# Regrouping the shared expert of a decoder layer into units of 320 and 384, with a warm-up and finer first loads

## The reference

```python
yg = xf @ shared_gw.T                      # shared expert, hidden size 704
y, g = jnp.split(yg, 2, axis=-1)
shared = jax.nn.silu(g) * y @ shared_dw.T
scores = jax.nn.sigmoid(xf @ gate_w.T)     # 8 experts, top 2 per token
for e in range(N_EXPERTS):                 # hidden size 352 each
    gu = xf @ up_w[e].T
    g_e, u_e = jnp.split(gu, 2, axis=-1)
    out = out + (silu(g_e) * u_e) @ down_w[e].T * we[:, None]
return shared + out
```

## Time and profile before

| | us |
|---|---|
| median of 3 runs | 1063.21 |
| the runs | 1061.88, 1063.21, 1064.40 |
| time of the profiled execution | 1066.47 |
| its span, first to last instruction | 1064.7 |

### The profile page before, as it was taken

The page is one execution under the profiler, slowest core; times in us unless marked ns, Lnnn a source line. Parts: engine busy times, 40 slices in busy tenths (PEclk is TensorE's granted clock), DMA queues, the critical chain, the costliest instruction groups (busy, mean ns, idle before and its releaser), DMA issues.

```text
span 1064.7 us, 20098 instructions
## 1 busy us (share of the span) xinstructions
PE 1019.2 (96%) x6978; PEld 905.5 (85%) x6978; DVE 704.2 (66%) x1454; ACT 524.1 (49%) x1033; POOL 530.5 (50%) x515
## 2 busy tenths in 40 slices
PE   6999888999999999999999999999999899999996
PEld 5866667899999999999999999999887788778785
DVE  4277776777777777767767767767786364455447
ACT  5355545555455455455455455455543245556510
POOL 0156866763643643643643644644572644454452
PEclk9999999999999999999999999999999999999999
DMA  8100104424323223233223333224210869999742
GB/s 294 60 31 2 60 16 138 150 111 149 120 111 115 98 109 114 97 108 114 99 107 114 101 107 112 101 107 150 93 69 1 333 253 370 395 380 380 279 134 83
DMA packets 44696, 153.45 MB, mean 144 GB/s; under 512 B 3704, under 2 KB 3704, under 8 KB 41568
## 3 DMA queue, kind: packets, MB, share of 16 engines
q1 hardware_dynamic: 42400, 145.38, 38.2%
q0 software_dynamic: 2240, 7.34, 2.1%
HBM read 130.04 MB, written 22.66 MB: 143 GB/s over the span
## 4 chain that ended last, share of the span: by engine, by line
PE 71%; POOL 4%; DVE 4%; issue 3%; ACT 1%; another core or an unknown queue 1%; POOLq 0%; DVEq 0%; ACTq 0%
PE xa_y_ps L86 6%; PE xa_y_ps L88 5%; PE xa_y_ps L87 5%; PE ex_raw_ey_ps L2092 5%; PE ex_raw_gu_ps L86 4%; PE ex_raw_gu_ps L88 4%; PE ex_raw_gu_ps L87 4%; PE xa_c_ps L1880 4%; PE xa_c_ps L1876 3%; PE xa_c_ps L1875 3%; PE xa_turn_ps L1957 3%; PE xa_turn_ps L1913 3%; PE front_k_ps L86 3%; PE front_k_ps L88 3%; PE front_k_ps L87 3%
## 5 line engine op out<-in xcount | busy, mean ns | idle before, releaser
L1221 POOL TENSOR_TENSOR xa_probs<-xa_probs,xa_inv_sum 112x750 f32<-112x750 f32 x63 | 97.9, 1553 | 75.6 <-DVE xa_inv_sum L1548 75.6
L1497 DVE TENSOR_TENSOR xa_kT_lo<-xa_turn_ps,xa_kT_hi 128x750 fp32r<-128x750 f32 x63 | 59.2, 940 | 99.9 <-ACT xa_kT_hi L1309 99.8
L1206 POOL TENSOR_TENSOR k_ms<-k_ss,sum_eps 125x6 f32<-125x6 f32 x63 | 12.6, 200 | 210.7 <-DVE k_ss L1513 210.7
L1875 PE MATMUL xa_c_ps<-xa_probsT_hi,xa_nat 125*128 125x224 f32 x384 | 92.3, 274 | 2.7 <-ACT xa_probsT_hi L1325 2.7
L1876 PE MATMUL xa_c_ps<-xa_probsT_hi,xa_nat 125*128 125x224 f32 x384 | 92.3, 275 | 0.0
L1209 POOL TENSOR_TENSOR k_inv<-k_ms,neg_half 125x6 f32<-125x6 f32 x63 | 83.5, 1326 | 8.3 <-POOL k_ms L1206 6.7
L1325 ACT CAST xa_probsT_hi<-xa_turn_ps 125x672 fp32r<-125x672 f32 x62 | 44.6, 720 | 87.2 <-PE xa_turn_ps L1957 87.2
L1331 ACT ACTIVATE xa_probs<-xa_scores_ps,xa_bias,xa_q_scale 112x375 f32<-112x375 f32 x126 | 82.8, 663 | 5.8 <-DVE xa_bias L1523 4.4
L1875 PEld LDWEIGHTS xa_c_ps<-xa_probsT_hi,xa_nat 125*128 125x128 f32 x384 | 73.6, 192 | 3.5 <-issue 3.1
L1876 PEld LDWEIGHTS xa_c_ps<-xa_probsT_hi,xa_nat 125*128 125x128 f32 x384 | 73.5, 191 | 0.5
L86 PE MATMUL front_k_ps<-land_xa_wk_hi,land_xa_ctx 128*125 128x256 f32 x252 | 71.4, 283 | 1.4 <-DVE front_k_hat L1540 1.0
(11 more groups left out here) (379 smaller groups left out, 3484.9 us busy)
## 6 DMA issues: line engine op xcount, KB each, us to landing
xa_nat<-ctx_split SPq DMA_DIRECT2D x56, 750.0 KB
ex_raw_raw<-in_w_units SPq DMA_DIRECT2D x15, 1408.0 KB, 7.9
ex_raw_raw<-in_w_units SPq DMA_DIRECT2D x15, 768.0 KB
land_ex_raw<-in_w_units SPq DMA_DIRECT2D x8, 1408.0 KB, 8.2
land_ex_raw<-in_w_units SPq DMA_DIRECT2D x8, 768.0 KB, 7.6
ctx_split<-xa_nat SPq DMA_DIRECT2D x8, 750.0 KB
sorted_x<-ex_raw_y_sb SPq DMA_DIRECT2D x7, 768.0 KB, 10.5
ex_raw_x_nat<-sorted_x SPq DMA_DIRECT2D x21, 256.0 KB, 8.3
```

Of the source, the lines that this page charges most:

```text
L1221: pool.tensor_tensor(probs[0:T, u % 2], probs[0:T, u % 2], inv_sum[0:T, u % 2, :].unsqueeze(2).broadcast_to([T, 2, KV]), ALU.mult).then_in ...
L1497: dve.tensor_tensor(kT_lo[:, :, 0:KV], turn_ps[:, :, 0:KV], kT_hi[:, :, 0:KV].bitcast(F32), ALU.subtract).then_inc(sem["kT_lo_done"], 1)
L1875: pe.matmul(c_view[:, c], nat[0:KT, u % 2, 0, at], probsT_hi[0:KT, :, cols], start=(t == 0), stop=False)
```

## The change

1. PE first makes 11 products of the identity with itself into a bank that is not yet used, as soon as the constants are set, and `xT` is loaded in eight pieces (chunk and token half) rather than four, each with its own semaphore.
2. The shared expert is cut into 320 + 384 rather than 352 + 352. Unit A has hidden tiles of 128, 128 and 64; the 64 gate columns and the 64 up columns of its last tile lie side by side in one stationary operand of 128 columns, so one group of 12 products per token half makes both. The gate comes out in PSUM rows 0 to 63 and the up in 64 to 127, and ACT writes the silu to rows 64 to 127. Unit B has three full tiles. Columns are stored interleaved (gate tile, up tile, gate tile, ...).
3. Unit B's up part is 768 wide for each chunk rather than 704, so it takes 3072 columns of the raw buffer, 256 more than `UP` had; they lie in what was `DOWN`. Its load waits, besides the old wait, for the down products of unit 19, which used that buffer. Its high copy is in a wide view of the same place as `up_hi`.
4. SP no longer loads up and down of units 1 and 2 together as soon as the owners are known: it loads up of unit 1, waits for the scatters of tiles 0 to 2, loads up of unit 2, waits for the other scatters, loads x of blocks 0 and 1, and then down of 1 and 2.

The core of the diff:

```diff
+WIDE = 2 * HPAD
+WIDE_W = DC * WIDE + HC * D
+HALF_P = P // 2
+FIRST_HID = SHARED - HPAD
...
+                for g in range(2):
+                    cols = slice(g * HT, (g + 1) * HT)
+                    sp.dma_start(xT_raw[:, c, cols], xT[:, c, cols]).then_inc(sem[f"xT_{c}_{g}_loaded"], 16)
...
+            wait(pe, "consts_set", 8)
+            for _ in range(11):
+                pe.matmul(y_ps[:, 0:P], ident[:], ident[:], start=True, stop=True)
             wait(pe, "wq_lo_done", 1)
...
+        UP_LAST, DOWN_LAST = slice(0, DC * WIDE), slice(DC * WIDE, WIDE_W)
+        def rows_of(unit, c):
+            return slice(HALF_P, P) if (unit, c) == (0, HC - 1) else slice(0, P)
...
                 if u > RING:
                     sp.wait_ge(xs["up_ready"], ups_before(u - RING + 1))
+                if u == LAST_U:
+                    sp.wait_ge(xs["y_ready"], downs_before(u - RING + 1))
+                    sp.dma_start(raw[u % RING][:, UP_LAST], w_last[:, UP_LAST]).then_inc(xs[f"up_{u % RING}_loaded"], 16)
...
-            for u in (1, 2):
-                unit = unit_of(u)
-                load_up(u, unit)
-                load_down(u, unit)
+            early = [unit_of(u) for u in (1, 2)]
+            load_up(1, early[0])
             for t in range(TILES):
                 sp.wait_ge(xs[f"scattered_{t}"], 32)
+                if t == 2:
+                    load_up(2, early[1])
             load_x(0)
             load_x(1)
+            for u in (1, 2):
+                load_down(u, early[u - 1])
...
-                act.activation(silu_g[0:m, (base + k) % 2, :], gu_ps[0:m, (base + k) % 2, 0, 0:HT], ACT.Silu)
+                act.activation(silu_g[rows, (base + k) % 2, :], gu_ps[0:P - rows.start, (base + k) % 2, 0, 0:HT], ACT.Silu)
...
-                for half in range(2):
-                    w = slice(half * HID + at, half * HID + at + m)
+                for half in range(1 if (base, c) == (0, HC - 1) else 2):
+                    w = slice((2 * c + half) * P, (2 * c + half + 1) * P)
```

More of the change, by code:

```diff
@@ L203, in expert_views @@
         with ExitStack() as es:
-            for n, shape, kind in front + [(raw, [2, UNIT_W], dt)] + blocks:
+            for n, shape, kind in front + [(raw, [2, WIDE_W], dt)] + blocks:
                 part = es.enter_context(nc.sbuf_tensor(f"ex_{raw}_{n}", [P] + shape, kind))[:]
@@ L1356, in up_high @@
                 for c in range(DC):
-                    act.copy(high[u % 2][:, c, :], raw[u % RING][:, c * CHUNK:(c + 1) * CHUNK]).then_inc(xs["up_hi_done"], 1)
+                    act.copy(high_of(u, c), raw[u % RING][:, up_cols(u, c)]).then_inc(xs["up_hi_done"], 1)
             def down_high(unit, u):
@@ L1363, in down_high @@
                     act.wait_ge(xs["y_ready"], TILES)
-                act.copy(down_hi, raw[u % RING][:, DOWN]).then_inc(xs["down_hi_done"], 1)
+                act.copy(down_hi, raw[u % RING][:, DOWN_LAST if u == LAST_U else DOWN]).then_inc(xs["down_hi_done"], 1)
             def silu(k, base):
-                m = HID_TILES[k % HC][1]
+                rows = rows_of(min(base, 1), k % HC)
                 act.wait_ge(xs["up_ready"], base + k + 1)
@@ L1371, in silu @@
                     act.wait_ge(xs["mul_done"], base + k - 1)
-                act.activation(silu_g[0:m, (base + k) % 2, :], gu_ps[0:m, (base + k) % 2, 0, 0:HT], ACT.Silu).then_inc(xs["silu_done"], 1)
+                act.activation(silu_g[rows, (base + k) % 2, :], gu_ps[0:P - rows.start, (base + k) % 2, 0, 0:HT], ACT.Silu).then_inc(xs["silu_done"], 1)
             def hidden_high(unit, k):
                 g, c = divmod(k, HC)
-                m = HID_TILES[c][1]
+                rows = rows_of(unit, c)
                 act.wait_ge(xs["mul_done"], k + 1 if unit == 0 else UPS + NB + k + 1)
@@ L1380, in hidden_high @@
                     act.wait_ge(xs["y_ready"], TILES)
[L1381 removed]
+                act.copy(h_hi[rows, c, g * HT:(g + 1) * HT], h_full[rows, k % 2, :]).then_inc(xs["h_hi_done"], 1)
             def block_x(j):
@@ L2043, in dense_down @@
                 cols = slice(t * P, (t + 1) * P)
-                for c, (_, m) in enumerate(HID_TILES):
-                    w = slice(c * D, (c + 1) * D)
-                    mm = three_products(pe, ey_ps[:, n % 2, :], h_hi[0:m, c, cols], h_lo[0:m, c, cols],
-                                        down_hi[0:m, w], down_lo[0:m, w], c == 0, c == HC - 1)
+                for c in range(HC):
+                    w, rows = slice(c * D, (c + 1) * D), rows_of(unit, c)
+                    mm = three_products(pe, ey_ps[:, n % 2, :], h_hi[rows, c, cols], h_lo[rows, c, cols],
+                                        down_hi[rows, w], down_lo[rows, w], c == 0, c == HC - 1)
                 mm.then_inc(xs["y_ready"], 1)
@@ L2190, in _ @@
                 turn_hidden(j)
-            last_hi = high[LAST_U % 2]
-            last_lo = low[LAST_U % RING][:, UP].rearrange("p (a n) -> p a n", a=DC)
+            last_hi = up_wide
+            last_lo = low[LAST_U % RING][:, UP_LAST].rearrange("p (a n) -> p a n", a=DC)
             pe.wait_ge(xs["up_lo_v"], 2 * (LAST_U + 1))
@@ L2266, with interleaved @@
     units = [unit(a["L0_ffn_up_w"][e].T, a["L0_ffn_down_w"][e].T) for e in range(EXPERTS)]
-    for s in range(SHARED // HID):
-        rows = slice(s * HID, (s + 1) * HID)
-        gu = np.concatenate([shared_gw[SHARED:][rows], shared_gw[:SHARED][rows]], axis=0)
-        units.append(unit(gu.T, shared_dw.T[rows]))
+    gate_up = np.stack([shared_gw[SHARED:].T, shared_gw[:SHARED].T], axis=1)
+    def interleaved(rows):
+        return np.concatenate([gate_up[:, :, c:min(c + P, rows.stop)].reshape(D, -1) for c in range(rows.start, rows.stop, P)], axis=1)
+    whole, half = FIRST_HID // P * P, FIRST_HID % P
+    up = np.concatenate([interleaved(slice(0, FIRST_HID)), np.zeros((D, CHUNK - 2 * FIRST_HID), shared_gw.dtype)], axis=1)
+    down = np.concatenate([shared_dw.T[:whole], np.zeros((P - half, D), shared_dw.dtype), shared_dw.T[whole:FIRST_HID]], axis=0)
+    units.append(np.concatenate([chunks(up).reshape(P, -1), chunks(down).reshape(P, -1)], axis=1))
+    last = np.concatenate([chunks(interleaved(slice(FIRST_HID, SHARED))).reshape(P, -1),
+                           chunks(shared_dw.T[FIRST_HID:]).reshape(P, -1)], axis=1)
     arrays = {
@@ L2283 @@
         "w_units": np.stack(units),
+        "w_last": last,
     }
```

61 lines of the change are left out of this document (33 added, 28 removed).

## The result

Over 20 executions of each kernel the median went from 1063.98 to 1066.76 us. The ratio is 1.0028, with a 95% interval of 1.0019 to 1.0037: slower by 3.0 us. The forecast was 3.0 us above the median, with 0.56 on slower by over 0.2%. One of the 20 executions of the changed kernel took 3530.59 us and is left out of the ratio; the others lie between 1063.59 and 1071.23. The total agrees with the forecast, but two of its terms were mis-sized, in opposite directions. So the parts are read one by one.

The account below looks back on a forecast made before the run. PE was taken to bound the kernel, with 71% of the chain. Start -1.1, front -3.7 and late load +7.8 sum to +3.0 us: 1066.2 against the median of 1063.21, range 1061.5 to 1070.0.

Parts of the forecast that it names:

- The late load: Around block 20, before unit B: unit 22's up load issues 10.2 us later, stalling PE 6.1, with clock +7.8 us.
- The start: First products: half pieces of xT save 0.6 us and a higher clock 0.5; -1.1 us, between -0.3 and -1.9.
- half a piece is 229 KB less to wait for: At the start: the first product waits for less of xT, 0.6 us sooner at 382 GB/s.
- The clock: At the start: added products raise the clock for the first nine real ones; taken as 0.5 us, ends 0 and 1.3.
- 11 take 1.7 us at the full clock and 3.3 at half, and end by 6.0: At the start: the 11 added products, priced from transposes, finish before the first real product at 8.4.
- The front: Unit A to block 0: 4.8 us fewer products, gain 5.4 less 1.7 for clock, -3.7 us; +1.5 to -5.4.
- at most 856.03 - 850.6 = 5.4 us can be gained here: Before block 0: PE turns x at 856.03, though x lands at 850.6; at most 5.4 us of slack.
- there is less to win in them: Unit A: if median runs have less hold on PE, it reaches x about when it lands; up to 1.5 us lost.
- The merged group costs what one group did: Unit A's up products: stationary width 96 or 128 makes no difference, so 24 products fewer save 4.8 us.
- rival 2: Unit A: PE arrives sooner but is held until 847.4 by late signals, front gains 0; +6.7 us, 1069.9; chance 0.18.
- Rival 4: End of unit B: the late silu signal goes, 4.1 us come back; -1.1 us, 1062.1; chance 0.18.
- SP's new order: Unit A to block 0: later loads of units 1 and 2 still fit; cost 0, without the cover 4 us.

Follow-up runs that it names:

- second pair: Second profiles of the unchanged kernel before and of the changed kernel, taken with the experiments; spans 1057.34 and 1064.07 us.
- e1: Changed kernel, but unit 22's up load in two pieces, the larger at its old place, only the last 256 columns waiting for unit 19; 1062.6 us, ratio 0.9971.
- e2: Kernel before, with only the wait for unit 19's down products added to unit 22's up load; 1072.76 us, ratio 1.0068.
- e3: Kernel before with the new start alone (11 added products, xT in half pieces); 1062.73 us, ratio 0.9971; run again 1056.44, ratio 0.9976.
- e7: e1 without the 11 added products, xT still in half pieces; 1060.46 us, ratio 1.0016 to the kernel before.
- e4: e1 with the old start and the old order of SP's first loads, leaving the regrouping; 1068.0 us, ratio 1.0019 to the kernel before.
- e6: e1 with the old order of SP's first loads; 1056.2 us, ratio 0.9976 to the kernel before; run again 1055.77, ratio 0.9975.
- second group: Experiments on clock, SP's order and warm-up, sharing executions: kernel before unchanged, median 1058.41 us; changed kernel run again, 1065.37, ratio 1.0063.
- third group: Experiments sharing executions with the kernel before (median 1058.68 us): that kernel unchanged again, 1059.02, ratio 1.0002, and e3 and e6 again, among others.

## Why the prediction was right, and where it was not

**The late load: right, step by step.** Predicted +6.1 us of stall and +1.7 of clock. Measured 8.66 - 2.66 = +6.0 and 33.26 - 32.12 = +1.1; in the second pair +5.9 and +1.6. (Against the 31.63 of e1, the same grouping without the stall, the clock takes 1.6 and 2.1.) e2 adds it alone, +7.2; e1 takes it away, and by the ratios 1.0028 and 0.9971 of two groups that is some -6. The landing, 6.48 us after the issue, had been put at 6.6. The row that gave it was the issue of unit 22's down in the kernel before, which already carried the new condition.

**The start: mechanism right, size off.** The term was -1.1 and measured -2.9 at the values stage, and -3.1 and -2.5 in e3's two runs. The first product came 1.5 us sooner for 0.6: "half a piece is 229 KB less to wait for" was priced at 382 GB/s, but the first half piece landed 3.9 us after its issue where the whole one took 5.8, and e7, with half pieces alone, starts at 7.31 too. The clock gave 1.3 for 0.5, the upper end of its range. The step that failed there is "11 take 1.7 us at the full clock and 3.3 at half, and end by 6.0". The price was read off transposes, and these are not transposes: each of the 11 shows as two instructions in the trace (20 of the 22 stand in the row shown), and together they run from 2.72 until the first real one starts at 7.44. So PE had no idle time ahead of the first real product, and the clock was up within 0.7 us of it. Nor is it quite so that "they delay nothing": the low part of xT that the first real product needs was ready at 6.93, and in e7 and in both profiles of e3 PE follows 0.15 us behind it. Here they cost some 0.4 us.

**The front: the term that failed.** It was -3.7, from a slack of 5.4 less 1.7 for the clock. The step that failed is "at most 856.03 - 850.6 = 5.4 us can be gained here", taken as the gain. The 24 products did take 4.8 us less (36.08 to 31.27). Three things stand against them.
- The slack was the hold of one kind of execution. The prediction named that ("there is less to win in them") and gave the case an end of +1.5, but summed the other. In the second profile of the kernel before, without the hold, PE's weight load waits 0.46 us for x and the slack is nil.
- "The merged group costs what one group did" is true of the up products and not of the down products behind them. The third tile of hidden rows now lies in partitions 64 to 127. In the timelines of PE and of its weight loads, changed kernel, second profile:

```profile
838.35 0.50 PE L89 MATMUL ex_raw_ey_ps<-land_ex_down_hi,ex_raw_h_hi 128*128 128x512 f32 x1 [0.19 <-DVE resid L1712]
...
840.26 0.39 PE L90 MATMUL ex_raw_ey_ps<-land_ex_down_hi,ex_raw_h_lo 64*128 64x512 f32 x1
840.50 0.39 PE L91 MATMUL ex_raw_ey_ps<-land_ex_down_lo,ex_raw_h_hi 64*128 64x512 f32 x1
840.82 0.50 PE L89 MATMUL ex_raw_ey_ps<-land_ex_down_hi,ex_raw_h_hi 128*128 128x512 f32 x1
841.16 0.39 PE L90 MATMUL ex_raw_ey_ps<-land_ex_down_hi,ex_raw_h_lo 128*128 128x512 f32 x1
...
840.82 0.19 PEld L89 LDWEIGHTS ex_raw_ey_ps<-land_ex_down_hi,ex_raw_h_hi 128*128 128x128 f32 x1 [0.37 <-issue]
```

  Where the rows change from 64 to 128 the weight load does not start under the product in front, and the starts lie 0.32 and 0.34 apart in place of 0.23. From 128 to 64 it is the same, so a token tile takes 840.82 - 838.35 = 2.47 us. In the kernel before, with 96 rows, it takes 2.06, from one tile's 96-row products to the next tile's (second profile):

```profile
847.11 0.40 PE L86 MATMUL ex_raw_ey_ps<-land_ex_down_hi,ex_raw_h_hi 96*128 96x512 f32 x1
...
849.17 0.40 PE L86 MATMUL ex_raw_ey_ps<-land_ex_down_hi,ex_raw_h_hi 96*128 96x512 f32 x1
```

  Over 7 tiles that is 2.9 us of PE's time. It is not added to the result in full: the tiles ahead of x's turn only shorten PE's wait for x, and the cost falls on the tiles behind it. The Trainium skill ("TensorEngine Tiling (Array Packing)", section "Key Properties") says that a change of tiling mode drains TensorE. The trace fits that, with 0.2 us for each change, but the edit changed the partition where the rows begin along with their number, and no run separates the two. The prediction did not look at the down products to ask.
- The low clock around PE's new gap costs 5.1 us in the first profile, 1.7 in the second and in e1, e4 and e6, and nothing in e6's second profile. The prediction took the 1.7 of the kernel before for all.

Measured, from unit A's first product to block 0's: 54.48 to 52.74 us in the first pair (-1.7), 49.94 to 51.44 in the second (+1.5). e4, which holds more than the front, gives +2.0 at the median, though its quick profile has 51.76 here. So the front's gain depends on the execution: with the hold there is some (e1 has 50.58, e3, which is not regrouped, 55.18), without it there is next to none. That lies nearer to rival 2, "the front gives nothing", than to the forecast, but its reason, that PE is held until 847.4 all the same, did not hold: the turn of x moved to 851.10.

**The end.** Rival 4 said that 4.1 us come back if the late signal goes. It did go in the first pair of profiles, for 3.6 us. But the kernel before does without it too (15.10 in its second profile), and e1 and e4 show it (19.11 and 18.89). The late load does not decide it either: e2 has that load and two late silus (2.85 and 3.82 us), e3's first profile is without the load and has none. So nothing ties it to the change; with one profile for each it cannot be ruled out that the changed kernel meets it less often.

**The sum as measured.** In the first pair of profiles: start -1.3 (the -2.9 less a spell of low clock, last section), front -1.7, blocks +0.4, late load +7.1, end -3.5, together +1.0 us. In the second: -2.6, +1.5, +0.4, +7.5 and 0.0, together +6.7. The 20 executions of each lie between the two, at +3.0. The mechanism and the size of the largest term, the late load, were right. That the sum hit +3.0 is luck as well: it took too little for the start and too much for the front, and with the executions of the second group it would have missed by nearly 4 us.

SP's new order was costed at 0. No ratio shows a gain or a loss by it; the profiles point to a loss of 1 us, in the landing of x (at e6). PE's signals that come late while POOL issues were called strange, and what makes them late stays open. For the silus the signal is all that ACT can have waited for, by the kernel's code. The add at 847.41 also waits for its tile's two scatters, whose landings the profile does not show, so there a late landing is not ruled out.

## What to carry to other kernels

A load that inherits a stricter wait costs what the last load under that wait shows, so look for an instruction that already has it: its issue time is the new one's. Split such a load, so that only the part that needs the wait has it. Before products are taken from the engine that sets the time, find what the next stage waits for in a second, quick execution: slack in front of a DMA may be nothing but another wait. And a product saved by halving the rows of a tile may be paid back in part at each change between 64 and 128 rows, here 0.2 us.

## What the runs showed of the hardware that was not expected

- A change of stationary rows between 128 (partitions 0 to 127) and 64 (partitions 64 to 127) costs PE 0.2 us here; one between 128 and 96 costs nothing (the starts stay 0.23 apart).
- Each 128x128 product of plain f32 by plain f32 shows as two instructions, and 22 of them took 5.1 us in the changed kernel's first profile and 4.6 in e3's.
- The same kernel had medians of 1065.54 and 1058.41 us in two groups of executions on one chip. Its two profiles put 4.5 of their 7.4 us of difference between unit A and block 0, and 3.5 behind unit B. In both places something that waits for PE is late while POOL issues indirect DMAs or within some 2 us after (silus by 1.45 and 3.77 us).
- The first profile of the changed kernel, and all six of the second and third group that have both the regrouping and half pieces of xT, show the clock low for about 3 us more, near 145 or near 780 us, where the kernel before keeps 1.00 with like waits. These are the windows of the changed kernel's first profile:

```profile
777.50:780.00 2.50, 1.77 (x11) 1.62 (x11) 2.46 (x7) 1.51 (x5) 1.37 (x2) 0.86 0.22 88
780.00:782.50 2.50, 2.50 (x13) 2.50 (x13) 0.87 (x3) 0.53 (x1) 2.34 (x2) 0.50 0.03 7
```

  It costs 1.6 us up to unit A (the values stage is 2.9 us sooner, unit A's first product only 1.3). e1, e2, e4 and both profiles of e3 do not have it. Why is open.
